# A two-layer graph network on one NeuronCore: where ScalarE's edge loop begins in its instruction stream, and when the node features are loaded

## The chip, the cores and the metric

The kernel runs on one core of a Trainium2 chip. The metric is the device time of one execution in microseconds (us). Lower is better. A core has five engines that each run an instruction stream of their own: PE (TensorE, matrix products), DVE (VectorE), ACT (ScalarE), POOL (GpSimd, here the issuer of indirect DMAs) and SP (SyncE, here the issuer of plain DMAs). They meet only at semaphores.

## What is computed

6,250 nodes with 128 features, 100,000 edges (src, dst). Cut to what matters:

```python
edge_index = jnp.stack([src, dst])
h = jnp.maximum(_layernorm(x), 0.0)
# layer net 1: two GATv2 layers with 3 heads of 128, self loops added, batch norm between
xl, xr = (h @ Wl + bl), (h @ Wr + br)                 # [n, 3, 128]
e = leaky_relu(xl[src] + xr[dst], 0.2)
score = einsum('ehd,hd->eh', e, att)                  # softmax over the edges of a dst node
out = segment_sum(alpha[:, :, None] * xl[src], dst)
...
x = x + relu(batchnorm(concatenate([h2, x_in]) @ W2 + b2))
# layer net 2: attention with 8 heads over the same edges, summed by src, layer norm
h = jnp.maximum(_layernorm(x), 0.0)
x = x + edge_attention(h, edge_index, ...)
```

## The kernel before

Stages follow each other, each in a block that all engines leave together:

- **Counting and ranking by dst** (`sort_by_dst`). Edge keys are counted, then ranked in 200 half steps on PE, DVE and ACT; each edge gets a slot. POOL writes the edge words to DRAM at those slots, one indirect DMA for 125 edges (`Records.write`, L650). Of 800 columns of edges, 640 go this way.
- **The placement** (`Placement`, `SortBySrc`), in the same block as the ranking. The last 160 columns by dst and 464 columns by src are placed with one-hot products on PE, fed by DVE (L875, L877) and ACT (L917). Between the two lies the ranking by src (DVE L786, L789; ACT L751). POOL goes on with its 640 writes beside all of it.
- **The first norm and the first table**, still in the same block. `norm_parts` makes its work for each engine: SP loads the 6,250 x 128 features (`load_nodes`, 3.2 MB, L1070 and L1072), DVE centres them (L1080, L1082), ACT squares them (L1114), DVE scales them (L1092), ACT, PE and DVE turn them. `table_parts` then multiplies them with the layer's weights (PE L1210, L1211) and SP stores the table that the edges gather from (L1196).
- **The edge loop of a GATv2 layer** (`gat_edges`), once for each layer. 464 groups of 256 edge slots, handled by a software pipeline (`pipeline`) of which 16 groups make one iteration of a hardware loop on PE, DVE, ACT and SP; POOL's part is written out. The first groups (32 for ACT) and the last lie outside the loop, so ACT runs 27 iterations and takes the branch back 26 times in each layer. In a group PE looks up the dst rows (L1382), DVE adds the gathered rows and weighs them (L1524, L1532), ACT sums each of six heads (L1474, an activation and a read of its accumulator), a softmax runs once in 8 groups (PE L1409, L1416, L1424; DVE L1615 among others), ACT scales the rows (L1458), PE sums them by node (L1395) and DVE adds these up (L1571).
- Between the layers a projection with a batch norm, after them the second network (`edge_attention`) and the last norm (`finish`).

Each engine's order within an iteration is the order of the stage list that is handed to `pipeline`. L125 is the line of the hardware loop itself: its register instructions and its branch (COMPARE_BRANCH). The two calls of `gat_edges` write the same instructions, and so ACT's loop body is the same twice, at two places of its stream.

Of the change's names: `cleared` is the semaphore by which DVE tells SP that the last, partly filled block of the feature area is zeroed; `loaded` counts the two feature loads; `sorted_src` says that the words placed by src are stored. `k.y2` and `k.node` are areas of SBUF. The placement works in the front part of `k.feat`, of which `k.y2` is the first 6,272 columns, and at the very end of `k.node`. The ranking works in `k.node`.

Of the kernel before, what the change touches and what calls it, by code (L numbers as in the profile page):

```python
# [15 lines left out]
P = 128  # L16
N, D = 6250, 128
# [5 lines left out]
NB = -(-N // P)  # L23
NPAD = NB * P
# [3 lines left out]
COLS = E // EC  # L28
# [61 lines left out]
def reused(j):  # L90

    return later(j)
# [4 lines left out]
    return value if isinstance(value, int) else eng.snap(value)  # L97

def pipeline(eng, groups, stages, unroll=2, number=False):  # L100

    ahead, behind = max(lead for lead, _ in stages), min(lead for lead, _ in stages)

    def at(turn, s):
        numbers = {}
        for lead, fn in stages:  # L110
            q = s + lead
            if isinstance(turn, int) and not 0 <= unroll * turn + q < groups:
                continue
            if not number:
                fn(turn + q // unroll, q % unroll)
                continue
            if q not in numbers:
                numbers[q] = snapped(eng, unroll * turn + q)
            fn(turn + q // unroll, q % unroll, numbers[q])

    first = -(-(unroll - behind) // unroll)
    last = (groups - ahead) // unroll
    for t in range(-ahead, unroll * first):
        at(t // unroll, t % unroll)
    with eng.Fori(first, last) as i:  # L125
        for s in range(unroll):
            at(i, s)
    for t in range(unroll * last, groups - behind):
        at(t // unroll, t % unroll)
# [135 lines left out]
def sort_by_dst(k, io, beside):  # L265
# [7 lines left out]
    nc = k.nc  # L273
# [128 lines left out]
    with nc.Block() as block:  # L402
# [51 lines left out]
    match = [k.bank[6 + n][:, 0:HALF * P] for n in range(2)]  # L454
    flip = [k.bank[n][:, 0:HALF * P] for n in range(2)]
    dst_moves, src_moves = beside.placements()
    norm_on_sync, norm_on_scalar, norm_on_tensor, norm_on_vector, wait_features = norm_parts(
        k, k.feat[:, -2 * COLS - 4 * P:-2 * COLS], k.y2, k.node[:, 0:NPAD], k.node[:, NPAD:2 * NPAD], io["x"], "0")
    table_on_sync, table_on_scalar, table_on_tensor, table_on_vector = table_parts(*layer_tables(k, io, 1))
    sorted_src = k.sem("r_sorted")  # L460
    R = CU
    with nc.Block() as block:
        @block.sync
        def _(sp):
            def load_keys(j, s):
                if s % 2:
                    return
                h = R * j + s
                if reused(j):
                    sp.wait_ge(ohT_ready, h - R + 2)  # L470
                sp.dma_start(lo_bc[s // 2], k.lo_edge[ds(h * (HALF * P), 2 * HALF * P)].partition_broadcast(P)
                             ).then_inc(bc_ready[s // 2], 16)

            pipeline(sp, halves, [(0, load_keys)], R)
            beside.on_sync(sp)
            src_moves.store(sp, k.moved_s, beside.moved_i)
            sp.sem_inc(sorted_src, 1)
            norm_on_sync(sp)
            table_on_sync(sp)

        @block.scalar
# [90 lines left out]
        @block.vector  # L572
        def _(dve):
            def high_rows(j, s):
                h = R * j + s
                if later(h, 2):
                    dve.wait_ge(looked, h - 1)
                    dve.wait_ge(multiplied, h - 1)
                one_hot_rows(hi3[s % 2], hi, snapped(dve, HALF * h), NB).then_inc(hi_set, 1)

            def key_columns(j, s):
                h = R * j + s
                if later(h, 4):
                    dve.wait_ge(looked, h - 3)
                dve.wait_ge(bc_ready[s // 2], 16 * j + 16)
                part = lo_bc[s // 2][:, s % 2 * HALF * P:(s % 2 + 1) * HALF * P]
                nc.vector.tensor_scalar(oh_loT[s % 4], part, k.part_f[:, 0:1], None, ALU.is_equal).then_inc(ohT_ready, 1)

            def split_table(j, s):
                h = R * j + s  # L590
                dve.wait_ge(coarse_set, h + 1)
                if later(h, 2):
                    dve.wait_ge(looked, h - 1)
                nc.vector.tensor_tensor(fine[s % 2], run[s % 2], coarse[s % 2], ALU.subtract).then_inc(fine_set, 1)

            def read_table(j, s):
                h = R * j + s
                dve.wait_ge(looked, h + 1)
                if later(h, 2):
                    dve.wait_ge(ranked, h - 1)  # L600
                nc.vector.tensor_tensor(prod[s % 2], look[s % 2][0:EC, :], oh_hi[s % 2], ALU.mult).then_inc(multiplied, 1)

            def slots(j, s):
                h = R * j + s
                dve.wait_ge(multiplied, h + 1)
                with nc.allow_low_precision(reason="a slot is a whole number below 2**24"):
                    nc.vector.tensor_reduce(pos_d[:, ds(HALF * h, HALF)], prod[s % 2].rearrange("p (u m) -> p u m", u=HALF),
                                            AX_X, ALU.add).then_inc(ranked, 1)

            pipeline(dve, halves, [(-1, read_table), (1, split_table), (2, key_columns), (-1, slots), (1, high_rows)], R)  # L610
            dve.wait_ge(ranked, halves)
            do = Order(dve, k.sem("r_order"))
            do(nc.vector.memset(k.lo_col[:, T_DST:TILES], 0.0))
            dst_moves.on_vector(dve, pos_d[:, DST_WRITTEN:], beside.word_dst[:, DST_WRITTEN:], k.lo_col[:, 0:T_DST])
            beside.on_vector(dve)
            src_moves.on_vector(dve, beside.pos_i[:, SRC_WRITTEN:], beside.word_src[:, SRC_WRITTEN:], beside.moved_i)
            dve.wait_ge(sorted_src, 1)
            norm_on_vector(dve)
            table_on_vector(dve)
# [475 lines left out]
def norm_parts(k, work, x, rows, scratch, load, tag):  # L1095

    nc = k.nc
    cut = Carver(work)
    mean, rstd = cut(NB), cut(NB)
    stage = [cut(P) for _ in range(2)]  # L1100
    names = ("loaded", "order", "sq_ready", "squared", "var", "rooted", "ready", "cleared")
    loaded, order, sq_ready, squared, var_ready, rooted, ready, cleared = (k.sem(f"n{tag}_{n}") for n in names)
    staged = [k.sem(f"n{tag}_staged{s}") for s in range(2)]
    turned = [k.sem(f"n{tag}_turned{s}") for s in range(2)]
    kept = [k.sem(f"n{tag}_kept{s}") for s in range(2)]

    def on_sync(sp):
        if load is not None:
            sp.wait_ge(cleared, 1)
            load_nodes(sp, load, x, loaded)  # L1110

    def on_scalar(act):
        act.wait_ge(sq_ready, 1)
        nc.scalar.activation(scratch, rows, ACT.Square).then_inc(squared, 1)  # L1114
        act.wait_ge(var_ready, 1)
        nc.scalar.activation(rstd, rstd, ACT.Sqrt).then_inc(rooted, 1)
        act.wait_ge(ready, 1)

        def relu(j, s):
            if reused(j):  # L1120
                act.wait_ge(turned[s], j)
            nc.scalar.activation(stage[s], rows[:, ds((2 * j + s) * P, P)], ACT.Relu).then_inc(staged[s], 1)

        pipeline(act, NB, [(0, relu)])

    def on_tensor(pe):
        def turn(j, s):
            pe.wait_ge(staged[s], j + 1)
            if reused(j):
                pe.wait_ge(kept[s], j)  # L1130
            nc.tensor.transpose(k.bank[s][:, 0:P], stage[s], k.ident[:, :]).then_inc(turned[s], 1)

        pipeline(pe, NB, [(0, turn)])

    def on_vector(dve):
        do = Order(dve, order)
        if load is not None:
            nc.vector.memset(x[:, (NB - 1) * D:NB * D], 0.0).then_inc(cleared, 1)
            dve.wait_ge(loaded, 32)
        center(k, do, dve, x, rows, scratch, mean, rstd, 1e-5, sq_ready, squared, var_ready, rooted)  # L1140
        scale_rows(k, rows, rstd).then_inc(ready, 1)

        def keep(j, s):
            dve.wait_ge(turned[s], j + 1)
            nc.vector.tensor_copy(k.hT[:, ds((2 * j + s) * P, P)], k.bank[s][:, 0:P]).then_inc(kept[s], 1)

        pipeline(dve, NB, [(0, keep)])
        do(nc.vector.tensor_scalar(rows, rows, 0.0, None, ALU.max)) if load is None else None

    def wait_features(eng):  # L1150
        for s in range(2):
            eng.wait_ge(kept[s], (NB + 1 - s) // 2)

    return on_sync, on_scalar, on_tensor, on_vector, wait_features

def by_head(v):
# [117 lines left out]
def gat_edges(k, att, tag, late):  # L1275

    nc = k.nc
    groups, U = GROUPS, 2 * CG
# [16 lines left out]
    first = [cut(1) for _ in range(2)]  # L1295
# [25 lines left out]
    with nc.Block() as block:  # L1321
# [119 lines left out]
        def _(act):  # L1441
# [37 lines left out]
                        act.wait_ge(turned, c - 1)  # L1479
                    nc.scalar.copy(score[s // CG], score_in[s // CG]).then_inc(scored, 1)  # L1480

            pipeline(act, groups, [(-3, exps), (-11, weight), (0, reduce)], U)

        @block.vector
        def _(dve):
# [792 lines left out]
```

## Time and profile before

| | us |
|---|---|
| median of 3 runs | 6345.56 |
| lowest, highest | 6339.74, 6350.01 |
| the profiled execution | 6317.56 |
| its span | 6315.4 |

The page gives, by engine, busy time and its share of the span, and the span in 40 slices of 158 us with the busy tenths of each engine. Stages by time of the span: counting to 222 us, ranking to 545, placement to 1182, norm and first table to 1341, first edge loop about 1390 to 2985, projection and second table to 3206, second edge loop to about 4995, then the second network. A wait is shown as idle time ahead of an instruction with what ended it; "issue" is idle time that ended with nothing that the profile shows. ACTq and SPq are the parts of an engine that take instructions from the stream; register and branch instructions are listed only there. The instruction queue (q14) carries the instruction streams themselves to the engines.

### The profile page before, as it was taken

Reading aid. Unit: us, or ns where it says so; the run is one execution under the profiler, and the core shown is the slowest. Engines: PE = TensorE matmul, PEld = TensorE weight load, DVE = VectorE, ACT = ScalarE, POOL = GpSimd, SP = SyncE. Lnnn points to the kernel's source line nnn. Section 1 sums busy time; section 2 is a strip of 40 time slices with the busy share of each in tenths; the row PEclk is TensorE's granted clock in tenths of the full one; section 3 lists DMA queues with packets and bytes.
Section 4 is the critical chain, followed back from the end, with each engine's and each line's share of the span. In section 5 each row is a group of like instructions: output and inputs, shape, how many; then the busy total and the mean of one; then the engine's idle time right before and its main releaser. Section 6 shows DMA issues by size and latency. Waiting matters only on the chain. (4 is left out here: it accounts for less than half of the span.)

```text
span 6315.4 us, 122309 instructions
## 1 busy us (share of the span) xinstructions
PE 4846.5 (77%) x22358; PEld 2873.2 (45%) x22359; DVE 5297.8 (84%) x12463; ACT 4432.6 (70%) x19858; POOL 4274.3 (68%) x3722
## 2 busy tenths in 40 slices
PE   3799689558988888888788888888888766666563
PEld 2575345234444444444644444444444445555552
DVE  9998898659999999999678898988888766666666
ACT  6487679429999999999278888888888553333332
POOL 0488777837777777776576676666666557777773
PEclk9999999779999999999899999999999977777776
DMA  0243000235555555556154444544445234444444
GB/s 16 54 86 30 2 2 2 31 116 144 140 139 140 137 141 139 140 139 114 27 152 130 125 129 127 131 124 127 129 125 124 42 106 130 128 129 128 129 129 77
DMA packets 342152, 657.19 MB, mean 104 GB/s; under 512 B 99030, under 2 KB 190100, under 8 KB 341506
## 3 DMA queue, kind: packets, MB, share of 16 engines
q0 software_dynamic: 191520, 481.83, 30.7%
q1 hardware_dynamic: 150370, 172.99, 10.7%
q14 instruction: 234, 1.92, 0.1%
q8 instruction: 28, 0.46, 0.0%
HBM read 618.58 MB, written 34.84 MB: 103 GB/s over the span
## 5 line engine op out<-in xcount | busy, mean ns | idle before, releaser
L1332 POOL DMA_INDIRECT feat_area<-xl_table,gather_col x1856 | 2178.9, 1174 | 948.3 <-issue 531.1
L1382 PE MATMUL bank<-node_area,feat_area 128*128 x3712 | 1481.2, 523 | 331.9 <-DVE feat_area L1524 146.2
L1458 ACT ACTIVATE feat_area<-feat_area 128x128 f32<-128x128 f32 x5104 | 1608.6, 419 | 145.8 <-issue 145.8
L1474 ACT ACTIVATE feat_area<-feat_area 128x130 f32<-128x130 f32 x5568 | 1500.4, 331 | 256.2 <-DVE feat_area L1532 254.4
L1395 PE MATMUL bank<-feat_area 128*128 128x390 f32 x3712 | 1433.4, 509 | 138.6 <-ACT feat_area L1458 90.2
L1382 PEld LDWEIGHTS bank<-node_area,feat_area 128*128 128x128 f32 x3712 | 646.9, 193 | 954.1 <-issue 701.7
L1474 ACT ACTIVATION_READ_ACCUMULATOR feat_area<-feat_area 128x1 f32 x5568 | 1054.3, 190 | 0.0
L1395 PEld LDWEIGHTS bank<-feat_area 128*128 128x128 f32 x3712 | 694.6, 195 | 694.8 <-issue 293.8
L2020 POOL DMA_INDIRECT feat_area<-kv_table,gather_src x832 | 808.1, 971 | 280.6 <-issue 252.1
L1524 DVE TENSOR_TENSOR feat_area<-bank,feat_area 128x780 f32<-128x780 f32 x928 | 890.0, 959 | 62.4 <-DMA feat_area<-xl_table,gather_col 43.8
L650 POOL DMA_INDIRECT word_by_dst<-feat_area,gather_col x640 | 791.8, 1237 | 195.0 <-issue 188.9
L1532 DVE SCALAR_TENSOR_TENSOR feat_area<-feat_area 128x780 f32<-128x780 f32 x928 | 889.8, 959 | 0.0
L2060 PE MATMUL bank<-feat_area 128*128 128x136 f32 x1664 | 362.1, 382 | 424.5 <-DVE feat_area L2131 423.7
L675 POOL DMA_INDIRECT word_by_src<-lo_src,gather_src x336 | 441.5, 1314 | 301.3 <-issue 146.4
L2073 ACT ACTIVATE feat_area<-feat_area 128x32 f32<-128x32 f32 x208 | 47.7, 229 | 734.5 <-DVE feat_area L2120 734.5
L2060 PEld LDWEIGHTS bank<-feat_area 128*128 128x128 f32 x1664 | 306.0, 267 | 473.6 <-DVE node_area L2146 326.7
L1571 DVE SCALAR_TENSOR_TENSOR node_area<-node_area,stays,bank 128x390 f32 x812 | 496.8, 612 | 15.5 <-PE bank L1395 15.3
L901 PE MATMUL bank<-feat_area 125*128 125x416 f16 (+1 forms) x2496 | 460.5, 347 | 7.9 <-ACT feat_area L917 4.8
L917 ACT ACTIVATE feat_area<-feat_area 125x128 f16<-125x128 f16 x1248 | 399.2, 390 | 75.2 <-DVE feat_area L875 64.2
L2107 DVE TENSOR_TENSOR feat_area<-feat_area,bank 128x512 f32<-128x512 f32 x208 | 143.1, 688 | 288.8 <-DMA feat_area<-kv_table,gather_src 284.2
L1063 DVE TENSOR_TENSOR feat_area<-iota_f,lo_col 128x256 f32<-128x256 f32 x928 | 384.6, 414 | 0.0
L901 PEld LDWEIGHTS bank<-feat_area 125*128 125x128 f16 x2496 | 243.6, 98 | 224.8 <-DVE feat_area L877 9.2
(363 smaller groups left out, 7140.4 us busy)
## 6 DMA issues: line engine op xcount, KB each, us to landing
feat_area<-lo_slot SPq DMA_DIRECT2D x464, 128.0 KB, 3.3
feat_area<-xl_table,gather_col POOLq DMA_INDIRECT x1856, 3.5
feat_area<-lo_slot_src SPq DMA_DIRECT2D x104, 256.0 KB, 3.4
node_area<-lo_edge SPq DMA_DIRECT2D x100, 256.0 KB
xl_table<-feat_area SPq DMA_DIRECT2D x98, 195.0 KB, 2.2
feat_area<-kv_table,gather_src POOLq DMA_INDIRECT x832, 2.8
feat_area<-gates SPq DMA_DIRECT2D x348, 32.0 KB
feat_area<-rowgates SPq DMA_DIRECT2D x696, 0.1 KB
```

The costliest lines, as they stand in the source:

```text
L650: pool.indirect_dma_start(k.word_d, bass.IndirectOffsetOnAxis(ap=self.pos[:, c:c + 1], axis=0), self.pair[:, c, :], None).then_inc(self.wr ...
L901: last = nc.tensor.matmul(self.out[p][m], sh.to_lane[s][:, p * P:(p + 1) * P], sh.to_tile[s][:, m * half:(m + 1) * half], start=False, sto ...
L1332: pool.indirect_dma_start(ring[:, at:at + HE], None, k.xl, bass.IndirectOffsetOnAxis(ap=rows, axis=0)).then_inc(gathered[s], 16)
L1382: last = nc.tensor.matmul(pair[s % 2][:, u, 0:HE], pick[s // 2 % 2][:, c:c + P], k.node[:, ds(columns[0], HE)], start=True, stop=True)
L1395: last = nc.tensor.matmul(sums_in[s % 2], place[s % 2][:, u * P:(u + 1) * P], ring[:, at:at + HE], start=u == 0, stop=u == GS - 1)
L1458: last = nc.scalar.activation(row[:, 0:D], row[:, 0:D], ACT.Copy, scale=row[:, D:D + 1])
L1474: last = nc.scalar.activation(at, at, ACT.Copy, accum_out=score_in[s // CG][:, to:to + 1])
L1524: nc.vector.tensor_tensor(z[s % V].rearrange("p (u e) -> p u e", u=GS), pair[s % 2][:, :, 0:HE], ring[:, s * W:(s + 1) * W].rearrange("p ( ...
L1532: nc.vector.scalar_tensor_tensor(out=zu, in0=zu, scalar=0.0, in1=att_w.unsqueeze(1).to_broadcast([P, GS, HE]), op0=ALU.max, op1=ALU.mult). ...
L1571: last = nc.vector.scalar_tensor_tensor(out=k.node[:, ds(to, HE)], in0=spare, scalar=k.stays[:, ds(g, 1)], in1=sums_in[s % 2], op0=ALU.mul ...
L2020: pool.indirect_dma_start(kv[s][:, u * KV:(u + 1) * KV], None, k.kv, bass.IndirectOffsetOnAxis(ap=rows, axis=0)).then_inc(gathered[s], 16)
L2060: last = nc.tensor.matmul(total[s % 2][u], place[s % 2][:, u * P:(u + 1) * P], wv[s % 2][:, u * VW:(u + 1) * VW], start=True, stop=True)
```

## The change

Second, the feature load. The memset of the last block and its `cleared` leave `on_vector` for a function of their own, which DVE calls right behind the ranking; SP issues the two loads right behind its key loads, ahead of `beside.on_sync`. The loads go to `k.node[:, NPAD:2 * NPAD]`, which the ranking used and the placement does not; the squares that ACT writes go to `k.y2` instead.

```diff
-def pipeline(eng, groups, stages, unroll=2, number=False):
+def pipeline(eng, groups, stages, unroll=2, number=False, head=None, hint=False):
-    with eng.Fori(first, last) as i:
+    with eng.bass.Fori(first, last, engines=(eng.engine,), head_slot=None if head is None else {eng.engine: head},
+                       hint_back_edge=hint) as i:
         for s in range(unroll):
             at(i, s)
-    norm_on_sync, norm_on_scalar, norm_on_tensor, norm_on_vector, wait_features = norm_parts(
-        k, k.feat[:, -2 * COLS - 4 * P:-2 * COLS], k.y2, k.node[:, 0:NPAD], k.node[:, NPAD:2 * NPAD], io["x"], "0")
+    norm_on_sync, norm_on_scalar, norm_on_tensor, clear_features, norm_on_vector, wait_features = norm_parts(
+        k, k.feat[:, -2 * COLS - 4 * P:-2 * COLS], k.node[:, NPAD:2 * NPAD], k.node[:, 0:NPAD], k.y2, io["x"], "0")
             pipeline(sp, halves, [(0, load_keys)], R)
+            norm_on_sync(sp)
             beside.on_sync(sp)
             src_moves.store(sp, k.moved_s, beside.moved_i)
             sp.sem_inc(sorted_src, 1)
-            norm_on_sync(sp)
             table_on_sync(sp)
             dve.wait_ge(ranked, halves)
             do = Order(dve, k.sem("r_order"))
+            clear_features(dve)
+    def clear(dve):
+        nc.vector.memset(x[:, (NB - 1) * D:NB * D], 0.0).then_inc(cleared, 1)
+
     def on_vector(dve):
         do = Order(dve, order)
         if load is not None:
-            nc.vector.memset(x[:, (NB - 1) * D:NB * D], 0.0).then_inc(cleared, 1)
             dve.wait_ge(loaded, 32)
-            pipeline(act, groups, [(-3, exps), (-11, weight), (0, reduce)], U)
+            pipeline(act, groups, [(-3, exps), (-11, weight), (0, reduce)], U, head=0)
```

## Rows read from the trace of the kernel before

**Rows 1.** The page's first part: busy time, share of the span, instructions.
```profile
PE 4846.5 (77%) x22358; PEld 2873.2 (45%) x22359; DVE 5297.8 (84%) x12463; ACT 4432.6 (70%) x19858; POOL 4274.3 (68%) x3722
```
**Rows 2.** Busy time by stretch: 25 iterations of the first edge loop, 25 of the second.
```profile
core 0: us, PE busy (x) PEld busy (x) DVE busy (x) ACT busy (x) POOL busy (x), PEclk, DMA share, GB/s
1559.30:2929.60 1370.30, 1219.16 (x3601) 606.06 (x3600) 1333.60 (x2800) 1301.94 (x7151) 1032.06 (x857) 1.00 0.53 139
3375.50:4892.40 1516.90, 1274.09 (x3601) 630.73 (x3600) 1336.19 (x2800) 1305.76 (x7151) 1023.29 (x857) 0.95 0.48 126
```
**Rows 3.** ACT's loop branch, first layer (window 1500 to 2960), then second (3370 to 4960).
```profile
L125 ACTq COMPARE_BRANCH  x26: 45/45/50, 1559.3 to 2929.6; - x26
...
L125 ACTq COMPARE_BRANCH  x27: 40/45/45, 3375.5 to 4959.0; - x27
```
**Rows 4.** ACT L1458: first layer's edge loop (1400 to 2900), then the second's (3300 to 5000), with its idle time.
```profile
L1458 ACT ACTIVATE feat_area<-feat_area x2359: 384/420/487, 1433.0 to 2899.8; 128x128 f32<-128x128 f32 x197
  issue: 5.3, 25
...
L1458 ACT ACTIVATE feat_area<-feat_area x2470: 384/422/526, 3301.3 to 4980.3; 128x128 f32<-128x128 f32 x190
  issue: 140.3, 52
```
**Rows 5.** ACT in order of time at one branch back of the second layer.
```profile
3435.13 0.20 ACT L1480 COPY feat_area<-bank 128x51 f32<-128x51 f32 x1
3438.13 0.40 ACT L1458 ACTIVATE feat_area<-feat_area 128x128 f32<-128x128 f32 x1 [2.80 <-issue]
3441.85 0.69 ACT L1458 ACTIVATE feat_area<-feat_area 128x128 f32<-128x128 f32 x2 [3.31 <-issue]
```
**Rows 6.** DVE L1615 in the second layer's loop (3300 to 4960), and what ended its idle time.
```profile
  PE bank L1425: 139.9, 26
```
**Rows 7.** The instruction queue: first layer's loop, second layer's, then 3435 to 3450 and 3450 to 3496.
```profile
q14 instruction: 10, 0.08, 0.0%
q14 instruction: 135, 1.11, 0.3%
q14 instruction: 3, 0.02, 0.6%
q14 instruction: 2, 0.02, 0.1%
```
**Rows 8.** ACT's groups of instructions in one iteration (3440 to 3500).
```profile
L1458 ACT ACTIVATE feat_area<-feat_area 128x128 f32<-128x128 f32 x88 | 27.9, 424 | 5.8 <-issue 5.8
L1474 ACT ACTIVATE feat_area<-feat_area 128x130 f32<-128x130 f32 x96 | 26.0, 338 | 3.6 <-DVE feat_area L1532 3.5
L1474 ACT ACTIVATION_READ_ACCUMULATOR feat_area<-feat_area 128x1 f32 x96 | 18.8, 197 | 0.0
```
**Rows 9.** SP and DVE in order of time behind the placement.
```profile
1176.14 0.59 DVE L885 SCALAR_TENSOR_TENSOR feat_area<-bank,node_area 128x416 int32<-128x416 f32 x1
1182.47 0.17 DVE L1138 MEMSET feat_area<- 128x128 f32 x1 [5.73 <-SPq L477]
1183.64 14.13 SPq L1072 DMA_DIRECT2D feat_area<-in_x  x1
1197.82 1.54 SPq L1185 DMA_DIRECT2D feat_area<-in_L_gnn_Wl  x1
1206.36 6.69 DVE L1080 TENSOR_REDUCE feat_area<-feat_area 128x49 f32<-128x6272 f32 x1 [23.73 <-DMA feat_area<-in_x]
```
**Rows 10.** Busy time by stretch: the placement's start, the load, the table behind POOL's end.
```profile
545.00:569.00 24.00, 20.47 (x91) 9.42 (x92) 20.16 (x65) 16.93 (x54) 19.12 (x17) 0.86 0.10 2
1182.00:1206.00 24.00, 0.00 (x0) 0.00 (x0) 0.17 (x1) 0.00 (x0) 19.13 (x17) 0.50 0.86 151
1282.00:1300.00 18.00, 18.00 (x57) 10.37 (x56) 7.78 (x14) 9.76 (x30) 0.00 (x0) 1.00 0.43 154
```
**Rows 11.** POOL's last record write, and ACT's last table copy that was listed.
```profile
1275.58 1.18 POOL L650 DMA_INDIRECT word_by_dst<-feat_area,gather_col  x1 [0.30 <-issue]
...
1336.17 0.48 ACT L1230 COPY feat_area<-bank 128x390 f32<-128x390 f32 x1 [0.83 <-PE bank L1211]
```

More of the change, by code:

```diff
@@ L1152, in wait_features @@
             eng.wait_ge(kept[s], (NB + 1 - s) // 2)
-    return on_sync, on_scalar, on_tensor, on_vector, wait_features
+    return on_sync, on_scalar, on_tensor, clear, on_vector, wait_features
 def by_head(v):
```

## Prediction

> **What bounds the kernel now.** The page's busy shares come first [rows 1]: DVE is the busiest engine with 84%, no engine is near 100%, so stages have different limits and each edit must be priced in its own stage. Then the busy time by stretch for the two edge loops, which together are half of the time [rows 2]. They run the same instructions: in 25 iterations of each, DVE 2800, PE 3601, ACT 7151, POOL 857. The first takes 1370.3 us, the second 1516.9. DVE is busy for 1333.6 us in the one and 1336.2 in the other, so the first loop is DVE's (97% of its time) and the second is held up by something else for some 147 us. The rows of ACT's branch give the period [rows 3]: first layer (2929.6 - 1559.3) / 25 = 54.81 us an iteration, second layer (4959.0 - 3375.5) / 26 = 60.90 us. (27 iterations make 26 branches back; the first layer's first branch lies outside the listed rows.)
>
> Where the second layer loses it is read from the waits. ACT L1458 sat idle for 140.3 us in 52 waits that end with "issue", against 5.3 us in the first layer [rows 4]: two waits for each of 26 iterations. In order of time they lie at the branch: after the last copy of an iteration 2.80 us pass to the first activation, then 3.31 us to the second [rows 5]. No semaphore ends them, and the second stands between two activations of one group, which wait for nothing. Engines are short of instructions there, and the instruction queue says the same: 135 packets in the second loop, 10 in the first [rows 7], and 3 + 2 = 5 in one iteration. 1.11 MB / 135 is 8 KB a packet.
>
> That this delay reaches the end is read from DVE: L1615 waits 139.9 us in 26 waits for PE's L1425, 5.4 us an iteration [rows 6]. PE's row sums (L1395) need ACT's scaled rows and stand ahead of L1425 in PE's order; DVE, in order too, stands behind L1615. So ACT's stall is handed through PE to DVE. [...]
>
> The third place is the start of the norm: DVE idles 23.73 us for the features [rows 9], with no PE and no ACT instruction in those 24 us [rows 10].
>
> **Edit 1, ACT's loop at a page's first slot.** It adds no work in the body. What it changes is how many fetched pieces the body covers. One iteration has 88 + 96 + 96 instructions in three groups [rows 8], a few more copies and exponentials and the register instructions; call it 300. By rows 7 the fetches are of one size, and in the second layer five are made in an iteration, in the first layer none of ACT's (10 packets for all engines in 25 iterations). The second stall comes one activation after the first: a piece ends just behind the loop's head there. So that body begins in the last slots of a piece, uses one piece for almost nothing, and needs one more than the engine keeps; the first layer's body happens to lie well. Beginning at a first slot is the layout that needs the fewest pieces for a given length, so it needs no more than the first layer's layout, and that one ran with no fetch. I take the first layer's period for both.
>
> [...]
>
> Sum: 26 iterations x 6.09 us = 158.4 us. From below the bound is the idle time that DVE shows for it, 139.9 us [rows 6], if the clock's part stayed. From above: nothing in the rows says that the second loop could be faster than the first; I allow 0.5 us an iteration, 171 us. I take 158, since the counts and DVE's busy time agree within 0.2% [rows 2]. When the stall goes, DVE is next, as it is in the first layer.
>
> Entering the loops: the engine jumps over padding. A jump to code that isn't there costs what the branch back costs now, 2.80 us, and 3.31 more if the piece behind is missing too [rows 5]; to code that is already there, nothing visible (the first layer's branches back). For two loops 0 to 12 us. ACT is nearly as busy as DVE (1301.9 of 1370.3), so little of it hides. I take one miss, 2.8 us. Code behind each loop shifts; other ACT loops are short and use few pieces wherever they begin: 0.
>
> **Edit 2, the feature load.** Removed from the path: DVE's wait of 23.73 us [rows 9] and the memset ahead of it, 0.17. DVE still waits for `sorted_src` (5.73 us, until 1182.47), which is untouched; then `loaded` is long reached and L1080 starts at once. Moved, each in its queue: on DVE the memset now stands at 545 us ahead of the placement, 0.17 us on a queue with 20.16 of 24 us busy [rows 10], at most 0.2 us. On SP the two loads, whose second issue holds SP for 14.13 us [rows 9], stand behind the key loads and ahead of the store of the src blocks; that store waits for DVE's work in the middle of the placement, more than 100 us later, so nothing waits for SP. The weight loads, issued at 1197.8 now, come at 1183: earlier, and the table needs them at 1266, so 0. The load itself runs at 86% of the DMA engines for about 22 us [rows 10]; at 545 to 569 us they are at 10%, and only POOL's record writes use them. Those made 17 steps in the 24 us of the load, exactly as many as in 24 us without it [rows 10], so the load costs POOL nothing. Reading the features from the other area changes no shape: 0.
>
> What is late next: POOL. Its last record write is at 1275.58 us, its landing some us behind, and the table's last copy at 1336.17 [rows 11]. With the chain 24 us earlier the table ends near 1313, still some 30 us behind POOL. More of the table now runs beside POOL; the table is held by PE (18.00 of 18 us busy) [rows 10], so I take 0, bound 3 us. Sum of edit 2: 23.9 - 0.2 = 23.7 us; bounds 18 and 24.
>
> **The sum.** 158.4 + 23.7 - 2.8 = 179.3 us. Against the profiled execution: 6317.56 - 179.3 = 6138.3 us. That execution lies 28 us under the median of the three runs and below all of them, by 0.4%; the stalls are as many in each run, so I take the same difference from the median: 6345.56 - 179.3 = 6166.3 us.
>
> **The rivals.**
> *The second loop finds another bound.* Without the stall the gathers must come at the first layer's rate, 139 GB/s against 126 now [rows 2]. The first loop does just that with the same count of POOL instructions, which speaks against it. With half of the gain left, 79 us: 6345.56 - 79 - 21 = 6246 us. Chance 5%.
> *The slot isn't where it says.* If the head lands elsewhere and the second body still covers a piece too many, only the load's gain remains: 6345.56 - 23.7 = 6322 us. Chance 5%.
> *Slower: the head's own piece is thrown out in each iteration.* If the engine drops the loop's first piece as soon as it reads ahead behind the last one, then where the head lies decides nothing that is good: a head at slot 0 could miss in both layers. It decides from the point where pieces used plus the one read ahead exceed what is kept. Each of 26 iterations of the first layer would then pay 6.09 us too: 6345.56 + 158.4 - 23.7 = 6480 us. Against it: the first layer's body, of the same length and not known to begin at a better slot, runs without it [rows 4, 7]. Chance 4%. [...]
> *The load hurts what it now runs beside*, or POOL becomes the end of the block: up to all of the 24 us lost, 6190 us. Chance 6%, inside the range.
> *The forecast*: 80%.
>
> **Range and chances.** The forecast's own bounds: most saved 171 + 24 = 195, so 6151; least 140 + 18 - 12 = 146, so 6200. With some us of spread between runs (10 us among three) I give 6147 to 6202, which takes in the fourth rival. The rest, 14%, lies outside, and a few per cent for what I don't see. A measurement of this kernel tells about 0.2% (13 us) from no change. Faster by more: the forecast and rivals one, two and four, 95%; within: 1%; slower: 4%.
>
> **What would show it.** Right: ACT's branch rows in the second layer 54.8 us apart; L1458 idle to "issue" under 10 us; some 10 packets on the instruction queue instead of 135; a clock of 1.00; L1615 without PE's 139.9 us; L1080 at about 1182.6 us with no wait for the features; the block's end near 1317 us. Wrong: a stall of 2.8 us left at the branch, or a first layer with over 55.5 us an iteration; DVE waiting for a gather in the second loop; POOL the last to leave the first block.

## The result and the profile after

| | before | after |
|---|---|---|
| median, us | 6345.50 (4 runs) | 6164.47 (4 runs) |
| lowest, highest | 6339.74, 6350.01 | 6154.68, 6168.87 |
| profiled execution's span | 6315.4 | 6162.2 |

The ratio is 0.9713, with a 95% interval of 0.9696 to 0.9730: 181 us less in the medians, against 179 forecast. The spans of the two profiles differ by less, 153 us. So what each edit gave is read from stages and not from this difference. It will turn out that one term of the sum was 8 us too large, and that another took 2 us too much off the gain.

The second edge loop first. The busy time by stretch of the changed kernel, 25 iterations of the first loop and then of the second, to be held against [rows 2]:

```profile
core 0: us, PE busy (x) PEld busy (x) DVE busy (x) ACT busy (x) POOL busy (x), PEclk, DMA share, GB/s
1557.20:2931.80 1374.60, 1219.22 (x3601) 606.45 (x3600) 1333.87 (x2799) 1302.81 (x7151) 1023.29 (x857) 1.00 0.54 139
3378.50:4750.20 1371.70, 1219.21 (x3601) 606.81 (x3600) 1334.43 (x2800) 1300.82 (x7151) 1029.88 (x857) 1.00 0.55 139
```

The same work as before, x7151 on ACT, now takes 1371.7 us in the second layer, 54.87 an iteration, and the first layer has not moved beyond its spread (54.98; 54.81 before; 54.84 in a second profile of the changed kernel). The clock is 1.00 in both, and DVE is busy for 97% of both: the bound that was forecast. ACT L1462, which answers to L1458 of [rows 4], in the second layer's block, and the instruction queue in the 25 iterations of its loop (135 packets in [rows 7]):

```profile
L1462 ACT ACTIVATE feat_area<-feat_area x2552: 384/420/513, 3252.6 to 4826.1; 128x128 f32<-128x128 f32 x197
  issue: 6.4, 27
```
```profile
q14 instruction: 10, 0.08, 0.0%
```

140.3 us of waiting for instructions have become 6.4. L1619, which answers to L1615 in [rows 6], has no idle time at all in the view of its line. Entering the loop, over the padding, is one branch and a short wait: L125 has a COMPARE_BRANCH of 38 ns in ACT's stream there (at 1502.0 and 3323.7 us), which the kernel before and experiment 2, without a `head`, have at neither place. The trace lists no slots and no pages. What the number given to `head` does is seen from such a branch and from experiments 5 to 7, where 71 or 72 makes 221 us. ACT in order of time at the first layer's entry (the second layer's wait is 0.42 us):

```profile
1501.95 0.20 ACT L1484 COPY feat_area<-bank 128x51 f32<-128x51 f32 x1
1502.60 0.69 ACT L1462 ACTIVATE feat_area<-feat_area 128x128 f32<-128x128 f32 x2 [0.44 <-issue]
```

The norm's start, DVE in order of time (compare [rows 9]):

```profile
1189.82 0.59 DVE L887 SCALAR_TENSOR_TENSOR feat_area<-bank,node_area 128x416 int32<-128x416 f32 x1
1195.47 6.69 DVE L1082 TENSOR_REDUCE feat_area<-node_area 128x49 f32<-128x6272 f32 x1 [5.06 <-SPq L479]
```

The 23.73 us for the features are gone: from the end of the placement to the first step of the norm it is 5.1 us instead of 29.6, and what is left is the wait for `sorted_src`. But this is not all that happened to the block. The waits between 1255 us (the table's weights) and the block's end at 1338, then the table's stores while POOL still writes (1262 to 1296; the last column is the time from issue to landing):

```profile
ACT feat_area L1234 <- DMA xl_table<-feat_area: 18.7, 13, 2.8
```
```profile
xl_table<-feat_area SPq DMA_DIRECT2D x17, 195.0 KB, 6.6
word_by_dst<-feat_area,gather_col POOLq DMA_INDIRECT x18
```

In the kernel before, ACT waited 2.1 us in that stage for stores, of which the median landed after 2.2 us. The stage is counted from DVE's first instruction on the weights to the end of the block. Before, that was 1266.3 to 1340.4, 74.1 us; it is now 1255.4 to 1338.0, 82.6 us (82.6 in a second profile too). So of 24.5 us gained at the norm's start 8.5 are given back in the table.

And the ranking, which the change does not touch, took longer in this profile. Busy time by stretch of the changed kernel: the ranking, then from its end to the end of the block, then the second edge loop's block from its start to a place in its last groups that lies behind all 26 branches back (PE x4061 in every kernel):

```profile
220.00:559.90 339.90, 308.40 (x5204) 237.80 (x5204) 320.15 (x1011) 260.42 (x600) 271.66 (x214) 0.99 0.44 79
559.90:1338.00 778.10, 627.81 (x2949) 324.29 (x2949) 624.20 (x1518) 546.17 (x1496) 583.59 (x476) 0.94 0.16 20
3210.10:4776.10 1566.00, 1379.38 (x4061) 685.82 (x4062) 1513.53 (x3167) 1465.27 (x8080) 1170.59 (x980) 1.00 0.55 140
```

Before, the same three were 324.8, 795.6 and 1721.6 us (ranking to 544.8, block's end 1340.4, second edge stretch 3207.3 to 4928.9). So the profiles differ by +15 in the ranking, -17.5 in the rest of the block, -155.6 in the second edge loop's stretch and about +5 between the two (first edge loop and projection): -153.

### The profile page after: what moved, and what is told of

It reads as the page before. It is cut to its first block and busy times, and to the rows that moved or that the text cites. A ratio compares the mean times of both kernels' runs of the same rounds, so it can differ in the third digit from the quotient of the medians.

```text
span 6162.2 us, 122312 instructions
## 1 busy us (share of the span) xinstructions
PE 4804.5 (78%) x22358; PEld 2857.0 (46%) x22359; DVE 5317.6 (86%) x12463; ACT 4428.8 (72%) x19858; POOL 4278.3 (69%) x3722
## 5 line engine op out<-in xcount | busy, mean ns | idle before, releaser
L1386 PE MATMUL bank<-node_area,feat_area 128*128 x3712 | 1455.8, 515 | 358.0 <-DVE feat_area L1528 154.1
L1462 ACT ACTIVATE feat_area<-feat_area 128x128 f32<-128x128 f32 x5104 | 1604.9, 418 | 12.8 <-issue 12.8
L1399 PE MATMUL bank<-feat_area 128*128 128x390 f32 x3712 | 1393.7, 498 | 19.6 <-issue 6.5
L1399 PEld LDWEIGHTS bank<-feat_area 128*128 128x128 f32 x3712 | 680.7, 190 | 557.9 <-issue 140.0
L652 POOL DMA_INDIRECT word_by_dst<-feat_area,gather_col x640 | 803.0, 1255 | 195.0 <-issue 191.4
L2064 PEld LDWEIGHTS bank<-feat_area 128*128 128x128 f32 x1664 | 303.5, 265 | 461.9 <-DVE node_area L2150 317.4
L2054 PE MATMUL bank<-node_area,feat_area 128*128 x1664 | 339.3, 373 | 14.4 <-ACT feat_area L2090 12.6
```

What stands on the lines that cost most here:

```text
L652: pool.indirect_dma_start(k.word_d, bass.IndirectOffsetOnAxis(ap=self.pos[:, c:c + 1], axis=0), self.pair[:, c, :], None).then_inc(self.wr ...
L1386: last = nc.tensor.matmul(pair[s % 2][:, u, 0:HE], pick[s // 2 % 2][:, c:c + P], k.node[:, ds(columns[0], HE)], start=True, stop=True)
L1399: last = nc.tensor.matmul(sums_in[s % 2], place[s % 2][:, u * P:(u + 1) * P], ring[:, at:at + HE], start=u == 0, stop=u == GS - 1)
L1462: last = nc.scalar.activation(row[:, 0:D], row[:, 0:D], ACT.Copy, scale=row[:, D:D + 1])
L2064: last = nc.tensor.matmul(total[s % 2][u], place[s % 2][:, u * P:(u + 1) * P], wv[s % 2][:, u * VW:(u + 1) * VW], start=True, stop=True)
```

## Experiments

Four questions: what each edit gives alone; whether the ranking's 15 us belong to the change; what it is about slot 0 that cures the stall; and whether POOL's writes are what slows the table. The runs of the first four were timed against 19 runs of the kernel before, with a median of 6329.52 us; the others have one timed execution each, beside one of the kernel before (6337.07; 6338.70 for slot 111 and for the hint without a slot).

**1. The first edit alone.**

```diff
 # the kernel before
-            pipeline(act, groups, [(-3, exps), (-11, weight), (0, reduce)], U)
+            pipeline(act, groups, [(-3, exps), (-11, weight), (0, reduce)], U, head=0)
```

> Before, with the first edit alone: ACT's edge loop begins at slot 0, the features are loaded where they were. If the second loop's stall is all that the edit removes, the second layer's period falls from 60.90 to about 54.9 us and the gain is 26 x 6.0 = 156 us, less at most 5 us for the entries: ratio 0.976. If the load edit gave the larger part of the 181 us between the medians, this stays above 0.985. In the trace L1462's counterpart L1458 has under 15 us of idle time to issue, and the instruction queue has about 105 packets instead of 234.

Measured: 6176.33 us, ratio 0.9752 (0.9723 to 0.9781). The line of ACT's scaling in the second layer's block, here L1459:

```profile
L1459 ACT ACTIVATE feat_area<-feat_area x2552: 385/416/494, 3270.5 to 4843.3; 128x128 f32<-128x128 f32 x197
  issue: 6.4, 27
```

The second edge stretch took 1564.6 us (3227.7 to 4792.3), and the instruction queue carried 105 packets in all instead of 234. The edit is worth 153 us by the medians and 157 by the ratio, whose interval (139 to 175) holds the 155.6 us of the stretch.

**2. The second edit alone.**

```diff
 # the changed kernel
-            pipeline(act, groups, [(-3, exps), (-11, weight), (0, reduce)], U, head=0)
+            pipeline(act, groups, [(-3, exps), (-11, weight), (0, reduce)], U)
```

> After, without the head: only the load stands beside the placement. Theory: the wait of 23.7 us goes, and the table's stores, now beside POOL's last record writes, give some 8 us back, so the first block is 15 to 16 us shorter than in a run with an equally long ranking: ratio 0.9975. Rival (the forecast's own term): 23.7 us, ratio 0.9963. Rival: nothing is left, because the ranking, 15 us longer in the profile of the changed kernel than in that of before, is longer for a reason that the load edit brings: ratio 1.000, and the ranking again takes about 338 us instead of 323. ACT's stall in the second loop stays, with 26 branches of about 2.8 us, or moves if the code ahead shifts it.

Measured: 6311.84 us, ratio 0.9968 (0.9956 to 0.9981), so 12 to 28 us. The interval holds 16 and 23.7 alike; what it rules out is that the edit gives nothing. The stages tell the two apart: from the ranking's end (556.6) to the block's end (1335.0) it is 778.4 us, against 795.6 in the profile before and 796.1 in experiment 4, so 17 to 18 us. (Experiment 1, with the load where it was, took 799.1; the second profile of the changed kernel 780.9.) The table stage again ran slower than before, 80.1 us, with 14.9 us of waits for stores:

```profile
ACT feat_area L1234 <- DMA xl_table<-feat_area: 14.9, 12, 2.1
```

The ranking took 337 us. ACT's stall in the second layer stayed as it was, and that layer's stretch took 1731.8 us:

```profile
  issue: 145.1, 52
```

**3 and 4. Both kernels once more.** No edit.

> The changed kernel once more, for a second profile. If the length of the ranking differs from run to run, this profile shows another value than 338 us for it (222 to 560 us of the span); if the change made it longer, it shows 338 again. Ratio 0.971 either way.

> The kernel before once more, for a second profile. Its first profiled execution, 6317.56 us, lies 28 us under the median of its runs. Theory: that execution was a quick one in a stage whose length varies with DMA waits, the ranking (323 us there) among them; this profile then lies nearer to 6345 and shows a ranking of 330 to 345 us. Rival: profiled executions are as quick as that one for a reason of the profiling: then it is near 6317 again. Ratio 1.000.

Measured: the changed kernel 6156.00 us, ratio 0.9724 (0.9695 to 0.9753), its ranking 332.3 us, the rest of the block 780.9 and the second edge stretch 1566.1. The kernel before 6323.40 us, ratio 0.9988 (0.9971 to 1.0005), its profile:

```profile
220.00:552.60 332.60, 306.91 (x5204) 237.23 (x5204) 321.58 (x1007) 260.73 (x600) 266.54 (x209) 0.99 0.58 80
552.60:1348.70 796.10, 626.84 (x2949) 324.83 (x2949) 621.38 (x1519) 546.24 (x1496) 589.95 (x481) 0.92 0.14 20
3216.60:4932.40 1715.80, 1434.66 (x4061) 710.24 (x4062) 1515.54 (x3167) 1471.20 (x8079) 1152.42 (x980) 0.95 0.49 129
```

The ranking differs from execution to execution: 325 and 333 us in the kernel before and 338 in experiment 1, all with the load where it was; 332 and 340 in the changed kernel and 323 to 338 in the others, all with the load moved. So nothing shows that the 15 us belong to the change. One thing that goes with a longer ranking was seen: DVE L587 (L588 in the changed kernel), one instruction of one shape, is slow or quick in it. Its group in the ranking, in the profile before, then in the changed kernel:

```profile
L587 DVE TENSOR_SCALAR node_area<-node_area,part_f 128x512 f16<-128x512 f16 x200 | 90.3, 452 | 4.0 <-DMA node_area<-lo_edge 4.0
```
```profile
L588 DVE TENSOR_SCALAR node_area<-node_area,part_f 128x512 f16<-128x512 f16 x200 | 112.7, 564 | 4.0 <-DMA node_area<-lo_edge 4.0
```

Most of the 200 take either about 0.34 or about 0.68 us, and both occur in every profile: over 0.5 us took 61 of them in the profile before and 128 in the changed kernel's. The slow ones come mostly in long runs of neighbours. The ranking's length does not follow their sum closely (115.5 us of it in the ranking of 333), and why it switches was not tried. That the kernel before has medians of 6345.5 and 6329.5 in two sets, with a profiled execution of 6317.56 in the first, is likewise left open; of my expectation for experiment 4 the ranking of 333 us came true, the time near 6345 did not (the profiled execution took 6320.38).

**5 and 6. Slots 71 and 72.** The trace lists 313 instructions between two of ACT's branches.

```diff
 # the changed kernel
-            pipeline(act, groups, [(-3, exps), (-11, weight), (0, reduce)], U, head=0)
+            pipeline(act, groups, [(-3, exps), (-11, weight), (0, reduce)], U, head=71)
```

and the same with `head=72`.

> After, with the loop's head at slot 71 instead of 0. Between two of ACT's branches the trace lists 313 instructions. Theory: a fetched piece holds 128 instructions (the packets are 8 KB), and the loop runs without fetches as long as it covers three pieces: slots 71 to 383 are three, so no stall, both layers near 55 us an iteration, time as with slot 0 (within 10 us). Rival, that the first slot of a page itself is what matters: stalls in both layers, some 300 us slower than with slot 0.

> After, with the head one slot further, at 72: slots 72 to 384 touch a fourth piece with the branch alone. Theory of three pieces of 128: each branch back now stalls in both layers, by the first layer 26 x 3 to 6 us and the second the same, so 150 to 320 us slower than with slot 0, and well over 300 packets on the instruction queue. [...]

Measured: 6144.63 us with slot 71, 6366.06 with slot 72. One slot is worth 221 us. That slot 71 is 11 to 20 us quicker than slot 0, and not within the 10 I expected, goes in part with its ranking of 323 us. Over 25 iterations of each loop, one takes 54.79 and 54.89 us in the two layers with slot 71, 58.81 and 58.76 with slot 72, where the stall is in both layers. ACT L1462 in the first layer's loop (1500 to 2930) with slot 71, then with slot 72, and the instruction queue over the whole span in the same order:

```profile
L1462 ACT ACTIVATE feat_area<-feat_area x2298: 384/420/490, 1499.8 to 2928.8; 128x128 f32<-128x128 f32 x192
  issue: 5.3, 26
```
```profile
L1462 ACT ACTIVATE feat_area<-feat_area x2152: 384/421/489, 1500.2 to 2929.3; 128x128 f32<-128x128 f32 x196
  issue: 97.4, 25
  PE bank L1399: 48.9, 16
```
```profile
q14 instruction: 105, 0.86, 0.1%
```
```profile
q14 instruction: 365, 2.99, 0.2%
```

365 - 105 = 260 packets for 2 x 26 branches back: 5 for each, as in the second layer before (234 - 105 = 129, again 5 for each of 26). From slot 72 the body of 313 reaches slot 384, that is 3 x 128, with its branch alone. So I take the pieces to be of 128 instructions: four of them are touched, and the fifth packet I take for one piece read ahead behind them, which the trace doesn't show apart. With three pieces touched nothing of ACT's is fetched in the loop: with slot 71 the queue has 10 packets for all engines in 25 iterations of the first layer (1555 to 2910 us), as many as in [rows 7]. Other sizes also have an edge at slot 384, but they do not make five packets: 64 would touch six pieces from slot 72, 192 three, and 96 five from slot 72 but four from slot 111 (experiment 7), where the packets are five all the same.

**7. Slot 111.** Four pieces again, with the next piece needed sooner behind the head.

```diff
-            pipeline(act, groups, [(-3, exps), (-11, weight), (0, reduce)], U, head=0)
+            pipeline(act, groups, [(-3, exps), (-11, weight), (0, reduce)], U, head=111)
```

> After, with the head at slot 111 of a piece of 128: four pieces as at slot 72, but the second piece is needed 17 instructions behind the head instead of 56. With the head at 72 there was one wait of 3.9 us at each branch and an iteration took 58.8 us. Theory: the second wait of the kernel before comes from needing the second piece before it can have arrived; 17 instructions are some 5 us of ACT's work, so the second wait is gone or short here, and an iteration takes 58.8 to 60 us. Rival: two waits come with every layout of four pieces and slot 72 was lucky: 60.9 us in both layers, some 320 us slower than with slot 0.

Measured: 6270.66 us, 56.98 and 57.00 us an iteration, and 366 packets, again five for each branch back. As expected there is only one wait of weight at the branch. That fits a head two instructions ahead of a piece's end in the kernel before ([rows 5]: one activation, then the second wait); where that head lay was not measured. But the iteration lies below my range, 58.8 to 60, since its one wait is shorter than slot 72's. (My 5 us for 17 instructions was too much as well: 313 take 55 us, so 17 take 3.) ACT in order of time at one branch, with slot 72 and with slot 111:

```profile
1612.51 0.20 ACT L1484 COPY feat_area<-bank 128x51 f32<-128x51 f32 x1
1617.12 0.69 ACT L1462 ACTIVATE feat_area<-feat_area 128x128 f32<-128x128 f32 x2 [4.41 <-issue]
```
```profile
1664.22 0.20 ACT L1484 COPY feat_area<-bank 128x51 f32<-128x51 f32 x1
1667.19 1.86 ACT L1462 ACTIVATE feat_area<-feat_area 128x128 f32<-128x128 f32 x6 [2.77 <-issue]
```

The instruction queue in these waits (1612.5 to 1617, then 1664 to 1667.2), and then with slot 111 ahead of the branch (1655 to 1657), goes with that:

```profile
q14 instruction: 2, 0.02, 0.9%
```
```profile
q14 instruction: 1, 0.01, 1.7%
```
```profile
q14 instruction: 1, 0.01, 2.4%
```

At this branch with slot 72 there is no packet in the 10 us ahead and there are two in the wait; with slot 111 one comes 7 us or more ahead of the branch and one in the wait. Pieces of 128 with one read ahead would explain it: with slot 72 the branch is the fourth piece's first instruction, so that entering this piece would order the one behind it, and the head's own piece would come after it; with slot 111 the order for reading ahead would have been given some 40 instructions earlier, 7 us at 313 instructions in 55 us. (The queue doesn't say which packet is which piece, so their order is argued and not shown.) So a badly placed head costs 2.1, 4.0 or 5.9 us an iteration, by where it lies (slot 111, slot 72, and the kernel before; all over 25 iterations, where the second layer before had 60.68 us).

**8 and 9. The hint.** The second new argument of `pipeline`, at slot 72 and with no slot asked for.

```diff
-            pipeline(act, groups, [(-3, exps), (-11, weight), (0, reduce)], U, head=72)
+            pipeline(act, groups, [(-3, exps), (-11, weight), (0, reduce)], U, head=72, hint=True)
```
```diff
-            pipeline(act, groups, [(-3, exps), (-11, weight), (0, reduce)], U, head=0)
+            pipeline(act, groups, [(-3, exps), (-11, weight), (0, reduce)], U, hint=True)
```

> [...]

> After, with no head slot but the hint on: the loop of the second layer lies where its four pieces stalled at every branch. With the hint at slot 72 the waits were gone and the instruction queue had 118 packets instead of 379, so that nothing was fetched again in the loop. Theory: the hint keeps the head's piece wherever it lies; this runs as the changed kernel does, 6145 to 6165 us, with 118 to 125 packets. Rival: the hint works only with a placed head; then the second layer keeps 5 fetches an iteration and the time is near 6312 us, that of the load edit alone.

Measured: 6156.06 and 6155.35 us, with 105 and 104 packets, 54.8 to 54.9 us an iteration in both layers and both kernels. Slot 72's 210 us are all gone, for one instruction an iteration:

```profile
L125 ACTq BRANCH_PREFETCH_HINT  x26: 31/31/31, 1552.3 to 2923.8; - x26
```

(The 118 and 379 packets in the last expectation take in 13 and 14 ahead of the span; the page counts 105 and 365.) For slot 72 with the hint I had estimated 55 to 59 us an iteration: of the waits in [rows 5] the first, 2.80 us, mostly gone, and up to 3 us left of the second. That gain was too small. No piece of ACT's is fetched at all in the loop: 10 packets for all engines between 1550 and 2925 us, as many as with slot 0. By what means is not shown.

**10. Fewer record writes.**

```diff
-        for c in range(DST_WRITTEN):
+        for c in range(DST_WRITTEN - 5 * DEEP):
 ...
-            pool.wait_ge(self.written[n], 16 * (DST_WRITTEN // DEEP))
+            pool.wait_ge(self.written[n], 16 * (DST_WRITTEN // DEEP - 5))
```

> After, leaving out the last 80 of POOL's 640 record writes (so 10,000 edge words are missing and the output is another), so that POOL ends near 1170 us instead of 1288, ahead of the table. Theory: the table's stores are slowed by the record writes beside them, so without these the table stage (L1242's wait to the end of the block) takes about 71 us instead of 80 as it did before the change, ACT's copies wait under 3 us for stores instead of 18.7, and a store lands in about 2.3 us instead of 6.6. Rival: the table is slower for another reason (the clock, the areas' places): 80 us again.

This kernel leaves out 80 of the 640 writes, so its output is not the right one; only its times are read. Measured: 6150.08 us, and POOL's last write at 1157 us. The table's stores between 1262 and 1296 us:

```profile
xl_table<-feat_area SPq DMA_DIRECT2D x26, 195.0 KB, 2.2
```

26 stores in that stretch instead of 17 (24 if the stretch begins as far behind the stage's start as in the changed kernel), landing in 2.2 us instead of 6.6, and no wait of ACT for a store was listed in the stage. From 1251.7 us to the block's end it is 74.8 us, as long as before the change (74.1) and 7.8 shorter than in the changed kernel (82.6). (The expectation's 71 and 80 are counted to the engines' last instruction; the end of the block is used here.) So the record writes beside the stores are the cause; by which way they slow a store was not tried.

## Why the prediction was right

- **The place and the mechanism of the stall: right.** ACT short of instructions, twice in an iteration of the second layer, handed through PE to DVE. With the stall gone all three views of it emptied together: L1462's waits, the packets, and DVE's wait.
- **26 iterations x 6.09 us = 158.4 us: right.** The second edge stretch fell by 155.6 us between the first two profiles; over six profiles, those of the two kernels and of experiments 1 and 2, it is 1715.8 to 1731.8 us with the stall and 1564.6 to 1566.1 without, so 150 to 167, and experiment 1 gave 139 to 175 by its interval. Taking the first layer's period rather than the 139.9 us of idle time was worth it: what an iteration lost beyond its 5.4 us of idle time (60.90 - 54.81 = 6.09 us in all) did come back, with the clock at 1.00, where it had been 0.95 [rows 2]. The granted clock behind the stall of [rows 5] was 0.50 from 3443 to 3449 us and 1.00 again from 3450; four matmuls of L1395 took 2.96 us there, against 1.57 us ahead of the stall. That it was the clock that made the part beyond the idle time isn't shown apart; PE's busy time in [rows 2], 1274 against 1219 us for the same instructions, speaks for it, but slot 111, with a clock of 0.98, loses less (2.1 us) than the 2.8 us of idle time at its branch.
- **"Beginning at a first slot needs no more pieces than the first layer's layout": right, for the reason given**, and slots 71 and 72 show the edge of it. The prediction did not know the size of a piece and did not need it.
- **Two readings of the branch rows were off, and cancel.** The first layer's branch that is missing from [rows 3] is the last one, at 2985.3 us, and not the first; and the 60.90 us take in a last interval of 66.6, without which the period is 60.68. Over all 26 intervals the layers took 1426.0 and 1583.5 us, 157.5 apart.
- **The entries, one miss of 2.8 us: too high.** Both were short waits, 0.44 and 0.42 us against the 2.80 us taken, so no miss was paid.
- **The load's wait, 23.7 us: right at its place, too large in the sum.** The term that failed is the sentence "More of the table now runs beside POOL; the table is held by PE (18.00 of 18 us busy) [rows 10], so I take 0, bound 3 us". It measured 8.5 us. I had compared POOL's pace with and without the load (17 steps in 24 us each) and found that POOL did not suffer, and asked who is late next; I had not asked what POOL's writes do to the stores that they now meet. The rows gave a warning: PE was busy for 18.00 of 18 us behind POOL's end only [rows 10], and POOL's last write lay at 1275.58 us [rows 11] with the table hardly begun, so they showed nothing of a table beside POOL. By the rest of the block (795.6, 796.1 and 799.1 us against 778.1, 780.9 and 778.4) edit 2 is worth 15 to 21 us, 18 in the mean. For the same reason the sign "the block's end near 1317 us" failed: it was 1338.0, of which 15 us are the longer ranking. L1082, which answers to L1080, began at 1195.5 us and not at 1182.6, but that is the ranking alone.
- **That the total met the median within 2 us is partly luck.** By the stages of the first two profiles the change is worth 155.6 + 17.5 = 173 us, by the means of three profiles each 157 + 18 = 175. The second set measured 173.5 (0.9724), the first 181, with intervals that overlap; the forecast of 179 stood between them. The medians of the kernel before lie 16 us apart in the two sets, which is more than the error of the term that failed, and the cause is open.
- **The rivals.** No other bound appeared in the second loop: the gathers ran at 139 GB/s. The slower rival, that a head's piece is thrown out by reading ahead, fits what slot 72 shows: five packets for each branch back where four pieces are touched, and a kernel that is 29 us slower than the one before beside it (one execution of each). At slots 0 and 71, with three pieces touched, there is no such packet. The fifth packet agrees with one piece read ahead, as its point of decision has it; that a piece read ahead throws out the head's was the author's estimate, and no run shows it.

## What to carry to other kernels

Where two loops with the same instructions run at different speed, compare idle time that ends in "issue" behind the loop's branch and the packets of the instruction queue: an engine that fetches its loop again shows it there. For a long ACT body, ask how many pieces of 128 instructions it touches from where it begins, keep that to three (three: no packet of ACT's in the loop, four: five for each branch back), and pin the head or use the hint; one slot more cost 221 us here. Loops of other lengths and of other engines were not tried. When a transfer is taken off the path, price the stage that moves forward as well: it now runs beside what it used to follow.

## What the hardware showed that was not expected

- An ACT body of 313 instructions fetched again costs 2.1, 4.0 or 5.9 us an iteration by its place; from slot 71 nothing, from slot 72 4.0.
- The branch hint removed it whole: 105 packets instead of 365, at 31 ns an iteration.
- POOL's record writes, 0.04 MB in 34 us, stretched the landing of 195 KB stores beside them from 2.2 to 6.6 us.
- The same f16 instruction of 128x512 on DVE (L587) took about 0.34 or 0.68 us, both within each execution, and in two executions of the kernel before 61 and 138 of its 200 took over 0.5 us.
